# The last 24 token tiles of a routed expert mixture, fetched, mixed and normalised inside the attention layer that follows it

## The chip, the cores and the metric

The kernel runs on one NeuronCore of a Trainium2 chip. The metric is the device time of one execution in microseconds (us). Below, a "tile" is 128 tokens (128 partitions x 128 features, float32), and a "batch" is four tiles.

## What is computed

A post-norm decoder of four layers over 8192 tokens (128 sequences of 64) of width 128. Each of its twelve sublayers ends with a layer norm of the residual sum. The change touches the third and the fourth sublayer:

```python
def _L0_ffn_ref(hidden_states, router_weight, w1, w2):
    ...
    probs = jax.nn.softmax(x @ router_weight, axis=-1)      # 8 experts
    ...                                                     # the top 2 of them keep their probs
    y1, y2 = jnp.split(jnp.einsum('th,ehf->tef', x, w1), 2, axis=-1)
    g = jax.nn.silu(y1) * y2
    o = jnp.einsum('tef,efh->teh', g, w2)
    out = jnp.einsum('teh,te->th', o, local_probs)
def _L1_attn_ref(hidden_states, Wq, Wk, Wv, Wo):            # 16 heads of 64, 4 key/value heads, causal
...
x = _layernorm(x + _L0_ffn_ref(...), axis=-1)
x = _layernorm(x + _L1_attn_ref(...), axis=-1)
```

## The kernel before

All engines are programmed by hand: each has its own instruction list per block, semaphores order them, and a new block starts when every engine has finished the one before. The rows of x live in SBUF (`X`, 64 tiles).

**The mixture** is `routed_experts("L0f", ...)`. Tokens are sorted by expert in three parts of 16, 32 and 16 tiles. For a part, GpSimd scatters the rows of `X` to HBM (`L0f_sorted_x`). Then come 53 expert blocks J of 512 rows (15 + 23 + 15), all written out without a loop: SyncE loads a block's rows and weights (`XB`, `WB`) three blocks ahead, TensorE turns the rows and makes the three first products (L1018, L1020, L1022), ScalarE takes silu, VectorE multiplies the two halves (L1355, twice a block), TensorE makes the second product (L1033), and ScalarE copies the result out and stores it in HBM (`L0f_sorted_y`). Block J's VectorE products free the banks that TensorE needs for the first products of block J+1.

**The tail** brings the results back. When the blocks of a part are stored, GpSimd gathers them, batch by batch: eight indirect DMAs a batch (two experts x four tiles, L959), then the root of the batch before (`root`, L946 and L948: 1/sqrt of the variance). For a batch, VectorE runs `tail_pair(b)`: the shift `nb` of batch b-1 (L1296, waits for that batch's root), two weighted sums a tile into `ACC` (L1304, waits for the gather of b), and the statistics (L1284, L1288). ScalarE writes the normalised rows to `X` (L1082). The table `step_after` says after which block's products VectorE runs which batch: `{25:0, 27:1, 30:2, 32:3, 42:4, 44:5, 47:6, 49:7, 52:8}`. Batches 9 to 15 come after the last block. Part 1 (the second part) holds batches 4 to 11.

**Side work** belongs to later layers (a mask and the statistics of the context, `side_rows` on SyncE and `side_work` on VectorE, L1271 to L1280): eight of its 16 pieces lie beside the blocks of the second part, eight beside the tail after the last block.

**The attention** is `grouped_attention()`. A block of its own loads its four weights and waits for them. Then `pipeline` runs one slot per tile T: scores of T, transposes, values and output product of T-1, while the fills (turning `XS`, making q, k, v) of a coming pair of tiles stand between them. GpSimd copies the rows of a pair to `XS` (L2218) and makes the roots. VectorE has the most to do after TensorE: maximum, shift, copies, the softmax sum and scaling, residual, statistics. The first 8 slots are written out, then 13 turns of a loop hold four slots each, then the rest is written out.

## Time and profile before

| what | value |
|---|---|
| median of 3 runs | 4301.33 us (4296.24 to 4304.2) |
| the profiled execution, its own time | 4300.37 us |
| its span | 4298.6 us |
| TensorE busy / VectorE busy | 3699.6 us (86%) / 3249.1 us (76%) |
| ScalarE busy / GpSimd busy | 2228.5 us (52%) / 1616.4 us (38%) |
| mixture's last block ends on TensorE | 1062.3 us |
| attention begins on TensorE | 1157.2 us |

Busy shares are averages over the whole span; which engine sets the pace differs by stage, so a change in one stage is read from that stage's own rows.

### The profile page before, as it was taken

How to read it: one execution, taken by the hardware profiler on the slowest of the kernel's cores; microseconds unless marked ns; L12 is line 12 of the kernel's file. 1: busy time of each engine (PE TensorE's matmuls, PEld its weight loads, DVE VectorE, ACT ScalarE, POOL GpSimd, SP SyncE). 2: the span in 40 equal slices, each digit the busy share in tenths (PEclk: the TensorE clock that was granted, in tenths of full speed). 3: DMA queues.
4: the chain of work that ended last, by engine and by line, in shares of the span. 5: the costliest groups of instructions: out<-in, count | busy, mean ns of one | idle time of the engine just before them, and what ended most of it. 6: DMA issues, size and time to landing. Idle time of an engine off the chain costs nothing. (4 is left out here: it accounts for less than half of the span.)

```text
span 4298.6 us, 137640 instructions
## 1 busy us (share of the span) xinstructions
PE 3699.6 (86%) x48696; PEld 2734.9 (64%) x48696; DVE 3249.1 (76%) x7860; ACT 2228.5 (52%) x4080; POOL 1616.4 (38%) x2677
## 2 busy tenths in 40 slices
PE   8997998688299998998996858998989687879986
PEld 6775677466177776776776636776764344457764
DVE  7996887344488887887995187997977577769975
ACT  4664553345244443666882445666864354535553
POOL 4663343665411111112454442332223244435544
PEclk9998997899599999999996988999999788989988
DMA  2011112587200000110001840000112000000001
GB/s 78 27 48 38 37 37 62 167 248 188 66 2 0 0 0 11 43 43 28 18 16 58 248 139 13 14 14 30 33 38 64 21 1 0 0 19 24 24 14 39
DMA packets 293808, 209.64 MB, mean 49 GB/s; under 512 B 51137, under 2 KB 272193, under 8 KB 293441
## 3 DMA queue, kind: packets, MB, share of 16 engines
q1 hardware_dynamic: 233760, 157.72, 12.8%
q0 software_dynamic: 12288, 25.19, 2.0%
q10 hardware_dynamic: 47520, 23.60, 1.8%
q8 instruction: 143, 2.34, 0.2%
q14 instruction: 97, 0.79, 0.1%
HBM read 122.49 MB, written 54.53 MB: 41 GB/s over the span
## 5 line engine op out<-in xcount | busy, mean ns | idle before, releaser
L1355 DVE TENSOR_TENSOR L0f_G<-L0f_SG,L0f_psH 128x512 f32<-128x512 f32 x106 | 73.0, 689 | 170.5 <-ACT L0f_SG L1099 127.8
L2224 POOL TENSOR_TENSOR L1a_rs<-L1a_ag,eps 128x1 f32<-128x1 f32 x64 | 12.1, 189 | 476.3 <-DVE L1a_ag L2384 476.3
L938 POOL DMA_INDIRECT L0f_sorted_x<-X,L0f_IDX x128 | 123.1, 961 | 94.1 <-DMA L0f_sorted_x<-X,L0f_IDX 35.7
L959 POOL DMA_INDIRECT L0f_YG<-L0f_sorted_y,L0f_IDY x128 | 124.4, 972 | 69.8 <-issue 35.9
L2311 PE MATMUL L1a_psO<-L1a_WO,L1a_OT 128*64 128x128 f32 x2048 | 125.9, 276 | 6.7 <-ACT L1a_OT L2335 5.7
L2245 PE MATMUL L1a_psF<-L1a_XT,L1a_WQ 128*128 128x256 f32 x512 | 130.8, 389 | 0.5 <-DVE L1a_KT L2200 0.5
L2311 PEld LDWEIGHTS L1a_psO<-L1a_WO,L1a_OT 128*64 128x64 f32 x2048 | 110.6, 137 | 25.2 <-ACT L1a_OT L2335 23.6
L1915 PE MATMUL L3a_psH<-L3a_UT,L3a_WG 128*128 128x512 f32 x128 | 80.9, 718 | 50.1 <-DVE L3a_G L2028 48.6
L1033 PEld LDWEIGHTS L0f_psO<-L0f_WB,L0f_G 128*128 128x128 f32 x848 | 102.9, 192 | 25.5 <-issue 25.5
L586 ACT ACTIVATE L3x_PT<-L3x_psP 128x512 f32<-128x512 f32 x128 | 69.6, 595 | 88.5 <-PE L3x_psP L521 88.5
L586 ACT ACTIVATE L0x_PT<-L0x_psP 128x512 f32<-128x512 f32 x128 | 69.5, 595 | 83.1 <-PE L0x_psP L521 83.1
L2245 PEld LDWEIGHTS L1a_psF<-L1a_XT,L1a_WQ 128*128 128x128 f32 x512 | 93.5, 192 | 23.2 <-DVE L1a_KT L2200 9.7
L1362 DVE TENSOR_TENSOR L1m_YB<-L1m_psO,L1m_WB 128x512 f32<-128x512 f32 x37 | 25.2, 684 | 104.9 <-PE L1m_psO L1033 104.9
L586 ACT ACTIVATE L0a_PT<-L0a_psP 128x512 f32<-128x512 f32 x128 | 69.5, 595 | 65.8 <-PE L0a_psP L521 65.8
L1033 PE MATMUL L0f_psO<-L0f_WB,L0f_G 128*128 128x128 f32 x848 | 103.1, 275 | 0.0
L586 ACT ACTIVATE L2a_PT<-L2a_psP 128x512 f32<-128x512 f32 x128 | 69.6, 595 | 63.3 <-PE L2a_psP L521 63.3
L2329 ACT ACTIVATE L1a_PR<-L1a_PR 128x1024 f32<-128x1024 f32 x64 | 67.6, 1057 | 63.5 <-DVE L1a_PR L2350 63.5
L2324 ACT ACTIVATE L1a_PT<-L1a_psP 128x512 f32<-128x512 f32 x64 | 38.2, 597 | 114.4 <-PE L1a_psP L2288 111.8
L2239 PE MATMUL L1a_psF<-W,L1a_XS 128*128 128x128 f32 x64 | 14.2, 305 | 95.0 <-POOL L1a_XS L2218 94.9
L1982 ACT ACTIVATE L3a_GG<-L3a_psH 128x512 f32<-128x512 f32 x64 | 36.6, 596 | 114.3 <-PE L3a_psH L1916 114.1
L586 ACT ACTIVATE L1x_PT<-L1x_psP 128x512 f32<-128x512 f32 x128 | 69.5, 595 | 45.3 <-PE L1x_psP L521 45.2
L378 POOL TENSOR_TENSOR L1x_rs<-L1x_mv,eps 128x2 f32<-128x2 f32 x32 | 6.2, 195 | 227.6 <-DVE L1x_mv L658 227.6
(684 smaller groups left out, 12996.0 us busy)
## 6 DMA issues: line engine op xcount, KB each, us to landing
L0f_WB<-in_w12a SPq DMA_DIRECT2D x53, 312.0 KB, 3.5
L0f_XB<-L0f_sorted_x SPq DMA_DIRECT2D x53, 256.0 KB, 4.0
L0f_sorted_y<-L0f_YB ACTq DMA_DIRECT2D x53, 256.0 KB
L1m_WB<-in_w12b SPq DMA_DIRECT2D x37, 321.0 KB, 4.0
L1m_XB<-L1m_sorted_x SPq DMA_DIRECT2D x37, 256.0 KB, 3.8
L1m_sorted_y<-L1m_YB ACTq DMA_DIRECT2D x37, 256.0 KB
L0f_sorted_x<-L0f_AC SPq DMA_DIRECT2D x27, 256.0 KB, 4.0
L1m_sorted_x<-L1m_AC SPq DMA_DIRECT2D x27, 256.0 KB, 3.6
```

The source lines that it names most:

```text
L586: nc.scalar.activation(PT[:, A.par, 4 * hb:4 * hb + 4, :], psP[:, hb], ACT.Copy).then_inc(S[done].sem, 1)
L938: nc.gpsimd.indirect_dma_start(out=sorted_x[p][:, :], out_offset=bass.IndirectOffsetOnAxis(ap=IDX[:, k, t:t + 1], axis=0), in_=X[:, t, :], ...
L959: nc.gpsimd.indirect_dma_start(out=YG[:, b % 4, k, t % TB, :], out_offset=None, in_=sorted_y[p][:, :], in_offset=bass.IndirectOffsetOnAxis ...
L1033: m = nc.tensor.matmul(psO[:, J % 2, t, :], G[0:f, J % 2, c, t * P:(t + 1) * P], WB[0:f, J % 4, at:at + D], start=c == 0, stop=c == 1)
L1355: nc.vector.tensor_tensor(G[0:f, J % 2, c, :], SG[0:f, c, :], up, ALU.mult).then_inc(S["g_ready"].sem, 1)
L1362: nc.vector.tensor_tensor(YB[:, J % 3], psO[:, J % 2], along(WB[:, J % 4, 514:514 + D], TB), ALU.add).then_inc(S["expert_out"].sem, 1)
L1915: nc.tensor.matmul(psH[:, c % 2, 0, :], WG[:, c * D:(c + 1) * D], UT[:, A.u, :], start=True, stop=True)
L1982: nc.scalar.activation(GG[:, c % 2, :], psH[:, c % 2, 0, :], ACT.Gelu_apprx_tanh).then_inc(S["gelu"].sem, 1)
L2245: m = nc.tensor.matmul(bank[:, 256 * j:256 * j + 256], WQ[:, 2 * k + j, :], XT[:, N.u, :], start=True, stop=True)
L2311: m = nc.tensor.matmul(psJ[64 * s:64 * s + 64, :], OT[:, s, c, :], WO[:, s, c, :], start=c == 0, stop=c == QC - 1, skip_group_check=True)
L2324: nc.scalar.activation(PT[:, 0:4, :], psP[:, 0], ACT.Copy).then_inc(S["pt_a"].sem, 1)
L2329: nc.scalar.activation(PR[:, T.par], PR[:, T.par], ACT.Exp, scale=scale).then_inc(S["probs"].sem, 1)
```

## The change

The mixture's tail now handles batches 0 to 9 only (`HERE = 10`). The last 24 tiles (`LATER = 24`, tiles 40 to 63) are gathered, summed, normalised and written to `X` one tile at a time in slots -3 to 27 of the attention, by a new class `LateRows` whose pieces stand at the end of each engine's slot. The attention's weights are loaded by SyncE at the end of its list in the mixture; the block that loaded them is gone, and TensorE waits for them before its first slot. All 16 pieces of side work lie beside the blocks. `step_after` becomes `{25:0, 27:1, 30:2, 32:3, 42:4, 44:5, 46:6, 48:7, 50:8, 52:9}`, and the pieces of side work follow blocks 16, 18, 20, 22, 24, 28, 31, 34 to 41 and 43. The attention's written-out part grows from 8 to 32 slots, and its loop has 7 turns.

```diff
+LATER, LATE_FIRST = 24, 32
-def pipeline(eng, slot, ahead=3):
-    first, turns = 8, 13
+def pipeline(eng, slot, ahead=3, first=8):
+    turns = (60 - first) // 4
...
+            HERE = NBATCH - LATER // TB if later is not None else NBATCH
...
-                    if at < BLOCKS:
+                    if at < BLOCKS and b < HERE:
                         step_after[int(at)] = b
-                    at += 2.5 if gated else 2
-            SIDES = NBATCH // 2
+                    at += (2.5 if p == 1 else 2) if gated else 2
+            free = [J for J in range(first[1] + 1, BLOCKS) if J not in step_after]
+            side_after = dict(zip(free[0:14:2] + free[14:], range(NBATCH))) if gated else {}
...
-                        if gated and p == 1 and k % 2 == 0 and k // 2 < SIDES:
-                            side_rows(k // 2)
-                    if gated:
-                        for b in range(SIDES, NBATCH):
-                            side_rows(b)
+                        if J + 1 in side_after:
+                            side_rows(side_after[J + 1])
+                    if later is not None:
+                        later.load_weights(sp)
...
+            def fetch(self, g, T):
+                j = self.tile(T, -3)
+                if j is None:
+                    return
+                t = TILES - LATER + j
+                if j == 0:
+                    for name in ("stored0", "stored1", "stored2"):
+                        g.wait_ge(S[name].sem, S[name].base)
+                self.made(g, "mix", j - 3)
+                for k in range(2):
+                    nc.gpsimd.indirect_dma_start(out=self.YG[:, j % 4, k, :], out_offset=None, in_=self.sorted_y[t >= self.edge][:, :],
+                                                 in_offset=bass.IndirectOffsetOnAxis(ap=self.IDY[:, k, t:t + 1], axis=0)).then_inc(S[f"gathered{j % 4}"].sem, 16)
+            def root(self, g, T):
+                j = self.tile(T, 2)
...
+                self.made(g, "in_stats", j + 1)
+                self.made(g, "late_rows", j - 3)
+                nc.gpsimd.tensor_tensor(self.rt[:, j % 4, 0:1], self.ag[:, j % 4, 1:2], eps[:, 0:1], ALU.add).then_inc(S["in_eps"].sem, 1)
+                self.made(g, "in_eps", j + 1)
+                nc.gpsimd.tensor_tensor(self.rt[:, j % 4, 1:2], self.rt[:, j % 4, 0:1], half[:, 0:1], ALU.pow).then_inc(S["in_rstd"].sem, 1)
+            def mix(self, dv, T):
+                j, a, b = self.tile(T, 0), self.tile(T, 1), self.tile(T, 3)
+                if j is not None:
+                    t = TILES - LATER + j
+                    self.made(dv, f"gathered{j % 4}", 32 * (j // 4 + 1))
+                    self.made(dv, "late_rows", j - 3)
+                    nc.vector.scalar_tensor_tensor(self.ACC[:, j % 4, :], self.YG[:, j % 4, 0, :], self.gate[:, 0, t:t + 1], X[:, t, :], ALU.mult, ALU.add).then_inc(S["own"].sem, 1)
+                if a is not None:
...
+                    nc.vector.bn_aggr(self.ag[:, a % 4, :], self.st[:, a % 2, :]).then_inc(S["in_stats"].sem, 1)
+                if j is not None:
+                    self.made(dv, "own", j + 1)
+                    nc.vector.scalar_tensor_tensor(self.ACC[:, j % 4, :], self.YG[:, j % 4, 1, :], self.gate[:, 1, t:t + 1], self.ACC[:, j % 4, :], ALU.mult, ALU.add).then_inc(S["mix"].sem, 1)
+                if b is not None:
+                    self.made(dv, "in_rstd", b + 1)
...
+                if j is not None:
+                    self.made(dv, "mix", j + 1)
+                    nc.vector.bn_stats(self.st[:, j % 2, :], self.ACC[:, j % 4, :]).then_inc(S["in_bn"].sem, 1)
+            def rows(self, act, T):
+                j = self.tile(T, 4)
...
+                self.made(act, "late_shift", j + 1)
+                nc.scalar.activation(X[:, TILES - LATER + j, :], self.ACC[:, j % 4, :], ACT.Identity, scale=self.rt[:, j % 4, 1:2], bias=self.nb[:, j % 4:j % 4 + 1]).then_inc(S["late_rows"].sem, 1)
...
-            with nc.Block() as block:
-                @block.sync
-                def _(sp):
-                    for d, s_ in ((WQ[:, :, :], io["wq"]), (WK[:, :, :], io["wk"]), (WV[:, :, :, :], io["wv"]), (WO[:, 0, :, :], io["wo"]), (WO[0:64, 1, :, :], io["wo"][64:128]), (WO[64:128, 1, :, :], io["wo"][0:64])):
-                        sp.dma_start(d, s_).then_inc(S["weights_in"].sem, 16)
-                    sp.wait_ge(S["weights_in"].sem, S["weights_in"].base + 96)
...
+                        later.root(g, T)
+                        later.fetch(g, T)
+                    pipeline(g, slot, 3, LATE_FIRST)
...
+                    pe.wait_ge(S["grouped_in"].sem, S["grouped_in"].base + 96)
+                    pipeline(pe, slot, 2, LATE_FIRST)
...
+                        later.rows(act, T)
...
+                        later.mix(dv, T)
```

`self.tile(T, back)` gives j = slot number - back, so a tile's gather stands in slot j-3, its sums in slot j, its statistics' aggregate in slot j+1, its root (GpSimd) in slot j+2, its shift in slot j+3 and its rows (ScalarE) in slot j+4.

Three places show how instructions move. The first is GpSimd at the start of the attention. Before, right after the branch into the block (the three copies are those of pairs 0, 1 and 2):

```order
L946 TENSOR_TENSOR L0f_rt<-L0f_ag,eps 128x4
L948 TENSOR_TENSOR L0f_rt<-L0f_rt,half 128x4
L870 UNCONDITIONAL_BRANCH
L2210 UNCONDITIONAL_BRANCH
L2218 COPY L1a_XS<-X 128x256 x3
L2224 TENSOR_TENSOR L1a_rs<-L1a_ag,eps 128x1
```

Now (`LYG` receives a late tile's two expert rows, `Lrt` is its root):

```order
L955 TENSOR_TENSOR L0f_rt<-L0f_rt,half 128x4
L878 UNCONDITIONAL_BRANCH
L2289 UNCONDITIONAL_BRANCH
L1432 DMA L1a_LYG<-L0f_sorted_y,rest_IDY 128x128 x2
L2298 COPY L1a_XS<-X 128x256
L1432 DMA L1a_LYG<-L0f_sorted_y,rest_IDY 128x128 x4
L2298 COPY L1a_XS<-X 128x256
L1432 DMA L1a_LYG<-L0f_sorted_y,rest_IDY 128x128 x4
L2298 COPY L1a_XS<-X 128x256
L2304 TENSOR_TENSOR L1a_rs<-L1a_ag,eps 128x1
L2306 TENSOR_TENSOR L1a_rs<-L1a_rs,half 128x1
L1441 TENSOR_TENSOR L1a_Lrt<-L1a_Lag,eps 128x1
```

Two gathers stand ahead of the first copy to `XS`, and four ahead of each of the next two.

The second is VectorE at the end of an attention slot. Before, from the residual sum of one tile to the maximum of the next slot:

```order
L2373 TENSOR_SCALAR X<-L1a_RB,L1a_ag,L1a_rs 128x128
L2379 TENSOR_TENSOR L1a_RB<-L1a_psO,X 128x128
L2381 BN_STATS L1a_st<-L1a_RB 128x6
L2384 BN_AGGR L1a_ag<-L1a_st 128x2
L2346 TENSOR_REDUCE L1a_mx<-L1a_psS 128x16
```

Now, in one of the slots with the full late work:

```order
L2458 TENSOR_SCALAR X<-L1a_RB,L1a_ag,L1a_rs 128x128
L2464 TENSOR_TENSOR L1a_RB<-L1a_psO,X 128x128
L2466 BN_STATS L1a_st<-L1a_RB 128x6
L2469 BN_AGGR L1a_ag<-L1a_st 128x2
L1451 SCALAR_TENSOR_TENSOR L1a_LACC<-L1a_LYG,rest_gate,X 128x128
L1455 BN_AGGR L1a_Lag<-L1a_Lst 128x2
L1458 SCALAR_TENSOR_TENSOR L1a_LACC<-L1a_LYG,rest_gate,L1a_LACC 128x128
L1462 SCALAR_TENSOR_TENSOR L1a_Lnb<-L1a_Lag,L1a_Lrt 128x1
L1465 BN_STATS L1a_Lst<-L1a_LACC 128x6
L2431 TENSOR_REDUCE L1a_mx<-L1a_psS 128x16
```

Five instructions of a late tile stand between the aggregate and the next maximum.

The third is VectorE at the end of the expert blocks. Before, from block 49's products to block 52's (the last):

```order
L1355 TENSOR_TENSOR L0f_G<-L0f_SG,L0f_psH 128x512
L1355 TENSOR_TENSOR L0f_G<-L0f_SG,L0f_psH 48x512
L1296 SCALAR_TENSOR_TENSOR L0f_nb<-L0f_ag,L0f_rt 128x4
L1304 SCALAR_TENSOR_TENSOR L0f_ACC<-L0f_YG,L0f_gate,X 128x128 x4
L1304 SCALAR_TENSOR_TENSOR L0f_ACC<-L0f_YG,L0f_gate,L0f_ACC 128x128 x4
L1284 BN_STATS L0f_st<-L0f_ACC 128x6 x4
L1288 BN_AGGR L0f_ag<-L0f_st 128x2 x4
L1355 TENSOR_TENSOR L0f_G<-L0f_SG,L0f_psH 128x512
L1355 TENSOR_TENSOR L0f_G<-L0f_SG,L0f_psH 48x512
L1355 TENSOR_TENSOR L0f_G<-L0f_SG,L0f_psH 128x512
L1355 TENSOR_TENSOR L0f_G<-L0f_SG,L0f_psH 48x512
L1355 TENSOR_TENSOR L0f_G<-L0f_SG,L0f_psH 128x512
```

Now, from block 50's products (the first row is the second of its pair) to those of block 52:

```order
L1364 TENSOR_TENSOR L0f_G<-L0f_SG,L0f_psH 48x512
L1305 SCALAR_TENSOR_TENSOR L0f_nb<-L0f_ag,L0f_rt 128x4
L1313 SCALAR_TENSOR_TENSOR L0f_ACC<-L0f_YG,rest_gate,X 128x128 x4
L1313 SCALAR_TENSOR_TENSOR L0f_ACC<-L0f_YG,rest_gate,L0f_ACC 128x128 x4
L1293 BN_STATS L0f_st<-L0f_ACC 128x6 x4
L1297 BN_AGGR L0f_ag<-L0f_st 128x2 x4
L1364 TENSOR_TENSOR L0f_G<-L0f_SG,L0f_psH 128x512
L1364 TENSOR_TENSOR L0f_G<-L0f_SG,L0f_psH 48x512
L1364 TENSOR_TENSOR L0f_G<-L0f_SG,L0f_psH 128x512
L1364 TENSOR_TENSOR L0f_G<-L0f_SG,L0f_psH 48x512
L1305 SCALAR_TENSOR_TENSOR L0f_nb<-L0f_ag,L0f_rt 128x4
```

Batch 7, which stood behind block 49, now stands behind block 48; batch 8 moves from block 52 to block 50, and batch 9 from after the blocks to block 52.

## Rows read from the trace of the kernel before

**Rows 1.** Busy time of each engine in three stretches: blocks, gap, attention.
```profile
core 0: us, PE busy (x) PEld busy (x) DVE busy (x) ACT busy (x) POOL busy (x), PEclk, DMA share, GB/s
960.00:1062.30 102.30, 102.29 (x560) 71.43 (x558) 50.87 (x147) 54.90 (x104) 52.80 (x58) 1.00 0.75 200
1062.30:1157.20 94.90, 0.00 (x0) 0.00 (x0) 39.55 (x209) 16.96 (x41) 59.23 (x69) 0.51 0.33 85
1183.22:1223.90 40.68, 40.68 (x711) 32.52 (x711) 35.72 (x55) 19.75 (x33) 4.41 (x12) 1.00 0.01 3
```

**Rows 2.** Timeline of TensorE: start, length, instruction, idle before and its releaser.
```profile
1042.88 1.02 PE L1020 MATMUL L0f_psH<-L0f_XT,L0f_WB 128*128 128x512 f32 x2
...
1058.56 3.73 PE L1033 MATMUL L0f_psO<-L0f_WB,L0f_G 128*128 128x128 f32 x32
1157.21 0.69 PE L2239 MATMUL L1a_psF<-W,L1a_XS 128*128 128x128 f32 x2 [94.92 <-POOL L1a_XS L2218]
```

**Rows 3.** Timeline of GpSimd: roots of batches 6, 7, 8, gathers, first copy.
```profile
1042.55 1.03 POOL L948 TENSOR_TENSOR L0f_rt<-L0f_rt,half 128x4 f32<-128x4 f32 x1
...
1054.67 1.03 POOL L948 TENSOR_TENSOR L0f_rt<-L0f_rt,half 128x4 f32<-128x4 f32 x1
1055.90 1.00 POOL L959 DMA_INDIRECT L0f_YG<-L0f_sorted_y,L0f_IDY  x1 [0.19 <-issue]
1057.21 0.96 POOL L959 DMA_INDIRECT L0f_YG<-L0f_sorted_y,L0f_IDY  x1 [0.30 <-issue]
...
1066.07 1.04 POOL L948 TENSOR_TENSOR L0f_rt<-L0f_rt,half 128x4 f32<-128x4 f32 x1
...
1156.76 0.73 POOL L2218 COPY L1a_XS<-X 128x256 f32<-128x256 f32 x2 [12.36 <-SPq L2209]
```

**Rows 4.** Timeline of VectorE: block products and the sums of batches 9 and 15.
```profile
1040.66 1.41 DVE L1355 TENSOR_TENSOR L0f_G<-L0f_SG,L0f_psH 128x512 f32<-128x512 f32 x2 [0.53 <-ACT L0f_SG L1099]
1044.00 0.69 DVE L1355 TENSOR_TENSOR L0f_G<-L0f_SG,L0f_psH 128x512 f32<-128x512 f32 x1 [1.93 <-ACT L0f_SG L1099]
...
1067.14 0.16 DVE L1296 SCALAR_TENSOR_TENSOR L0f_nb<-L0f_ag,L0f_rt 128x4 f32<-128x4 f32 x1 [3.45 <-POOL L0f_rt L948]
1067.46 1.14 DVE L1304 SCALAR_TENSOR_TENSOR L0f_ACC<-L0f_YG,L0f_gate,X 128x128 f32<-128x128 f32 x4 [0.16 <-DMA L0f_YG<-L0f_sorted_y,L0f_IDY]
...
1139.41 1.14 DVE L1304 SCALAR_TENSOR_TENSOR L0f_ACC<-L0f_YG,L0f_gate,X 128x128 f32<-128x128 f32 x4
```

**Rows 5.** Timeline of VectorE: one whole step of the tail, batch 7.
```profile
1046.03 0.15 DVE L1296 SCALAR_TENSOR_TENSOR L0f_nb<-L0f_ag,L0f_rt 128x4 f32<-128x4 f32 x1
1046.10 1.13 DVE L1304 SCALAR_TENSOR_TENSOR L0f_ACC<-L0f_YG,L0f_gate,X 128x128 f32<-128x128 f32 x4
...
1048.44 0.87 DVE L1284 BATCH_NORM_STATS2 L0f_st<-L0f_ACC 128x6 f32<-128x128 f32 x4
1049.35 0.38 DVE L1288 BATCH_NORM_AGGREGATE L0f_ag<-L0f_st 128x2 f32<-128x6 f32 x4
```

**Rows 6.** Timeline: the mixture's last rows on ScalarE, the weights' first load on SyncE.
```profile
1144.73 1.65 ACT L1082 ACTIVATE X<-L0f_ACC,L0f_nb,L0f_rt 128x128 f32<-128x128 f32 x4 [3.66 <-DVE L0f_nb L1296]
...
1147.34 0.35 SPq L2171 DMA_DIRECT2D L1a_WQ<-in_wq  x1
```

**Rows 7.** Who waited for whom, 1180 to 1690 us: total, times, longest.
```profile
DVE L1a_OT L2358 <- PE L1a_psO L2302: 33.3, 61, 0.9
```

**Rows 8.** The attention's maximum on VectorE by tile: durations, first, last; its waits.
```profile
L2346 DVE TENSOR_REDUCE L1a_mx<-L1a_psS x64: 1191/1224/1226, 1168.7 to 1683.0; 128x16 f32<-128x1024 f32 x64
...
  issue: 4.4, 13
```

**Rows 9.** By tile or line, min/median/max: sums, mask work (ns), gathers' landing.
```profile
L1304 DVE SCALAR_TENSOR_TENSOR L0f_ACC<-L0f_YG,L0f_gate,X x64: 334/343/360, 932.4 to 1140.2; 128x128 f32<-128x128 f32 x64
...
L1271 DVE TENSOR_SCALAR maskk<-L0f_MK x16: 258/281/348, 890.5 to 1144.6; 128x256 bf16<-128x256 int32 x16
...
DMA to landing us min/median/max: 2.5/3.2/5.0
```

More of the change, by code:

```diff
@@ L825, in routed_experts @@
             RK, RS, MV = mem.sb("RK", [P, GT, NE]), mem.sb("RS", [P, GT, NE]), mem.sb("MV", [P, max(PARTS), NE])
-            carry, counts, gate = mem.sb("carry", [P, NG + 1, NE]), mem.sb("counts", [P, len(PARTS), NE]), mem.sb("gate", [P, top, TILES])
+            carry, counts = mem.sb("carry", [P, NG + 1, NE]), mem.sb("counts", [P, len(PARTS), NE])
+            gate = later.gate if later is not None else mem.sb("gate", [P, top, TILES])
             PLACE, MOVE = mem.sb("PLACE", [P, top, TILES]), mem.sb("MOVE", [P, TILES])
-            IDX, IDY = (mem.sb(n, [P, top, TILES], mybir.dt.uint32) for n in ("IDX", "IDY"))
+            IDX = mem.sb("IDX", [P, top, TILES], mybir.dt.uint32)
+            IDY = later.IDY if later is not None else mem.sb("IDY", [P, top, TILES], mybir.dt.uint32)
+            if later is not None:
+                later.sorted_y = sorted_y[-2:]
+                later.edge = part_tile[-2]
             CNT, NBK, ENDS, SH = (mem.sb(n, [P, NE]) for n in ("CNT", "NBK", "ENDS", "SH"))
@@ L1355, in _ @@
                                 nc.vector.tensor_tensor(G[0:f, J % 2, c, :], SG[0:f, c, :], up, ALU.mult).then_inc(S["g_ready"].sem, 1)
[L1356 to L1358 removed]
+                            if J in side_after:
+                                side_work(side_after[J])
                         else:
@@ L2213, in slot @@
                         N, A = T + 2, T - 2
+                        later.all_rows(g, T)
                         if T.par == 0 and N.ok:
@@ L2342, in slot @@
                         A, E = T - 1, T - 2
+                        later.all_rows(dv, T)
                         if T.ok:
@@ L2398, in build @@
                   bo=R("L0xb"), cross=True, norm="rms")
-        routed_experts("L0f", 2, "w12a", "rwa")
-        grouped_attention()
+        rest = Memory(nc, "rest")
+        later = LateRows(rest)
+        routed_experts("L0f", 2, "w12a", "rwa", later=later)
+        grouped_attention(later)
+        rest.close()
         attention("L1x", Wm("L1xq"), Wm("L1xk"), Wm("L1xv"), Wm("L1xo"), bq=C("L1bq"), bk=C("L1bk"), bo=rowb[:, 0, :],
```

74 lines of the change are left out of this document (50 added, 24 removed).

## The prediction

> **What bounds the kernel now.** I read the stage windows first. In the last 100 us of the expert blocks TensorE is busy throughout; then it does nothing for 94.9 us, with its granted clock down to 0.51; in the attention it is busy all the time again at clock 1.00 [rows 1]. TensorE's timeline says the same at the edges: its last block instruction ends at 1062.29, its next starts at 1157.21, and the releaser is GpSimd's copy to `XS` [rows 2]. So whatever shortens this gap comes off the end, and whatever lengthens an attention slot is added to it.
>
> What fills the gap is read from GpSimd, the engine that is busiest in it (59.2 us of 94.9) [rows 1]. A gather's start follows the last by 1.26 us (a busy 0.96 and 0.30 of issue), and a batch's eight gathers with its root take some 11.3 us: the roots of batches 6, 7 and 8 end at 1043.6, 1055.7 and 1067.1 [rows 3]. Batches 9 to 15 follow each other at this pace, VectorE's sums of batch 9 start at 1067.46 and those of batch 15 at 1139.41 [rows 4], and ScalarE's last rows end at 1146.38 [rows 6]. Then SyncE starts the weights' loads at 1147.34 [rows 6] and the first copy to `XS` at 1156.76 has waited for them [rows 3].
>
> In the attention VectorE is busy 35.7 of 40.7 us [rows 1]. Its one regular wait is for TensorE's value product before the copy to `OT`: 33.3 us in 61 slots, 0.55 us each [rows 7]. A slot takes (1683.0 - 1168.7) / 63 = 8.16 us [rows 8]. VectorE thus has about 0.55 us to spare in a slot, plus little.
>
> **Removed: batches 10 to 15 and the weights' block.** GpSimd's chain up to the gather of batch 9 stays where it is. VectorE's step for batch 9 then starts at 1067.46 as before, held by the root of batch 8 and the landing of the gather [rows 4]. From the start of a last batch's sums to the end of ScalarE's rows it took 1146.38 - 1139.41 = 6.97 us (sums, statistics, root, shift, rows) [rows 4, 6]. So the mixture ends at 1067.46 + 6.97 = 1074.4. Changing blocks takes 1147.34 - 1146.38 = 0.96 us [rows 6], which gives 1075.4. Now two gathers of 1.26 us stand ahead of the first copy: 1077.9. TensorE starts 0.45 us behind the copy (1156.76 to 1157.21) [rows 2, 3]: 1078.4. That is **78.8 us** earlier than 1157.21. The next two copies have four gathers ahead of them each (5 us). TensorE turned pair 1 more than 11 us after pair 0, because pair 0's fills lie between, so the second is hidden; the third waits for the sums of slot 0 and two gathers, and I give it 4 us of room; should it be late, each us counts once.
>
> **Moved: weights and side work beside the blocks.** The weights' loads are issued after the last block's operands, with more than 20 us before TensorE asks for them; taken as nothing. Eight more pieces of side work fall behind blocks 34 to 43; a piece has a mask conversion of 0.28 us [rows 9] and four statistics and aggregates like those of a tail step, 0.87 + 0.38 us [rows 5], so some 1.6 us. VectorE is busy 50.9 of 102.3 us there, and the window's 560 matmuls, 26 a block, make a block 4.8 us [rows 1]. A pair of block products may be late: the pair of block 48 ran at 1040.66 to 1042.07, behind a tail step, and TensorE's product of block 49, which needs it, began at 1042.88 without a wait [rows 2, 4]. Block 49's own pair began at 1044.00 [rows 4], so block 48's was due at 1039.2; to be done before 1042.88 and before the following product's need at 1043.7, the pair can begin as late as 1042.1, 2.9 us late. 1.6 us of side work fits. But it brings 384 KB more DMA into a period of 4.8 us (80 GB/s on top of 200, where the DMA share is 0.75 already [rows 1]), which can delay the store of the second part's last block, and with it all gathers. I take 1 us; bounds 0 and 4.
>
> **Moved: tail steps two blocks apart instead of 2.5.** VectorE's order puts a wait inside the blocks. Two blocks last 9.6 us, GpSimd's batch 11.3 us. Step 7 now stands behind block 48 (products due at 1039.2 to 1041.3), but needs the root of batch 6 (1043.6 [rows 3]) and the gather of batch 7, whose last DMA starts 1.5 us ahead of that root's 1042.55 and lands 2.5 to 5.0 us after its start [rows 3, 9], so at 1043.6 to 1046. So it starts at about 1045 and lasts 3.7 us (1046.03 to 1049.73 [rows 5]), until 1048.7. Block 49's products, due at 1044.0 [rows 4] and free to be 2.9 us late, push TensorE by 1.8 us. Step 8 behind block 50 waits likewise to 1057 and ends at 1060.8; block 51 (due at 1053.6 + 1.8) pushes 2.5 us more. The blocks end about 4.4 us later, at 1066.7. VectorE's step for batch 9 cannot start before 1067.4 anyway, so this is hidden by GpSimd's chain, with under 3 us of room on VectorE (block 52's second product pair ends at 1064.5). Cost 0; were the cover gone, each further us of slip counts once. Bounds 0 and 5.
>
> **Added: the late tile in a slot.** On VectorE: two sums at 1.13 / 4 = 0.28 us, statistics at 0.87 / 4 = 0.22, aggregate 0.10, shift 0.07 to the next start, and two dependent starts at 0.04 [rows 5]: 1.04 us a slot, for 24 slots (four more have only a part). If VectorE's waits for the value product close entirely, a slot grows by 1.04 - 0.55 = 0.49 us. If none is absorbed, it is 1.04, or 25 us; if VectorE also wins its small gaps, 0.35, or 8 us. The copies that VectorE makes for TensorE come later too, and TensorE then waits for some of them, but both grow by the same slot. I take 0.5: **+12 us**. On ScalarE one activation of a tile (1.65 / 4 = 0.41 us [rows 6]) joins 19.8 busy us of 40.7 [rows 1]: nothing. GpSimd gets two gathers and a root, 2.5 + 1.1 us, in a slot where it is busy 0.9 us: nothing. A tile's gather is issued three slots (24 us) before its sums, and lands within 5 us [rows 9].
>
> **Loop turns.** VectorE waited 4.4 us for issue at 13 turns [rows 8], 0.34 us each; six turns fewer, and part of it was TensorE's slack: -1 us (bounds 0 and -2).
>
> **Sum.** -78.8 + 1 + 12 - 1 = -66.8 us. Against the profiled execution's 4300.4 us this is 4233.6; the median of the runs shown is 0.9 us above that execution, well inside their scatter of 8 us. I predict 4234 us.
>
> **A rule that speaks against it.** Beside the gathers, VectorE's sums took 334 to 360 ns and the mask's conversion 258 to 348 ns [rows 9]: GpSimd's gathers hold VectorE up by no more than 0.09 us. The Trainium skill (SBUF — State Buffer, "Who interferes with whom") says that VectorE and GpSimd share a port pair as an exclusive lock, so that an instruction with two SBUF inputs, or a copy in a two-port mode, and a GpSimd instruction block each other for their whole length. By that rule each gather could hold VectorE for its 0.96 us; the rows here do not show it for gathers, and I keep their durations.
>
> **Rivals.**
> - *All of the late work lands on the path* (0.8 to 1.1 us a slot): VectorE becomes the bound and TensorE's fills wait for its copies, which wait behind the late work. For it: VectorE is already at 88% in a slot. Against it: the 0.55 us of wait. 4300.4 - 78.8 + 19 to 26 = 4241 to 4248 (the other two terms cancel). Chance 0.17.
> - *Cheaper than I think* (0.15 to 0.35 a slot): 4 to 8 us instead of 12, 4225 to 4230. Chance 0.09.
> - *The blocks slip beyond their cover* (side work's DMAs, two late steps): 3 to 8 us are exposed, 4237 to 4242. Chance 0.08.
> - *GpSimd's gathers block VectorE* in its long two-input multiplication: up to 2 x 0.96 us a slot, 24 slots: 46 us, 4280. Rows 9 speak against it. Chance 0.04.
> - *Slower: the gather comes too late for its sums.* If GpSimd, held by its waits for statistics and sums at a slot's end, issued a tile's gathers only one slot ahead of need, VectorE would stand in every slot for two gathers and a landing, 2.5 + 1.5 to 4 us. From 78.8 / 24 = 3.3 us a slot on, the gain is gone; at 4.5 it is 4300 + 30 = 4330. Against it: the waits in slot c ask for what VectorE made in slot c-1, and 24 us of lead. Chance 0.03.
> - *No gain*: the start of the attention stays bound by something that the gap hid. Nothing in the rows shows one. Chance 0.01.
>
> **How the numbers follow.** The forecast, 4229 to 4241, has 0.58. The 8-in-10 range takes in the cheaper case, the slipping blocks and the full price of the late work: 4224 to 4251. A measurement of this kernel can tell about 0.2% (9 us) from no change. "Slower" is 0.03; no gain is the same, and so is a small part of the blocking case at its worst: 0.02. The rest, 0.95, is faster.
>
> **What would show it.** TensorE's idle time before the first `XS` turn falls from 94.9 to about 12 us, with the turn at about 1078. VectorE shows waits for roots or gathers behind blocks 48 and 50, of 2 to 4 us. In the first 24 slots the period is 8.6 to 8.7 us, VectorE's wait before `OT` is all but gone, and later slots are back at 8.16. The prediction is wrong if the turn comes after 1085, if the period is beyond 9.2, or if VectorE waits for `LYG`.

## The result, and the profile after

The changed kernel takes 4257.7 us (median of 4 runs, 4250.0 to 4259.4) against 4301.2 us before: a ratio of 0.9896 with a 95% interval of 0.9879 to 0.9914. It is faster by about 44 us, or 1.0%. The prediction had said 67 us (4234, range 4224 to 4251), so the sign was right and the time lies outside the range. The profiled executions stand at 4300.37 and 4259.36 us, 41.1 us apart in their spans.

Windows of the changed kernel, with the columns of [rows 1]: the last expert blocks, the gap, attention slots with late work, slots without.
```profile
960.00:1077.34 117.34, 110.86 (x588) 75.92 (x586) 75.00 (x275) 60.03 (x116) 59.48 (x67) 0.97 0.83 227
1077.34:1094.80 17.46, 0.00 (x0) 0.01 (x1) 0.85 (x7) 5.43 (x13) 3.59 (x5) 0.61 0.11 31
1114.00:1300.00 186.00, 176.86 (x3046) 140.39 (x3046) 175.55 (x338) 90.56 (x161) 77.74 (x135) 1.00 0.06 17
1340.00:1600.00 260.00, 257.87 (x4560) 207.02 (x4555) 229.40 (x350) 123.52 (x209) 28.97 (x80) 1.00 0.00 1
```
The gap of 94.9 us [rows 1] is down to 17.5, but the blocks now end at 1077.3 instead of 1062.3. In the slots with late work VectorE is busy 175.55 of 186 us, and TensorE is no longer busy all the time.

TensorE's timeline in the changed kernel: its first instruction of the mixture, blocks 51 and 52, the first turn of `XS`, and the first instruction after the attention.
```profile
706.25 0.69 PE L980 MATMUL L0f_psX<-W,X 128*128 128x128 f32 x2 [6.85 <-DMA L0f_TRI<-in_tri]
...
1069.31 2.08 PE L1029 MATMUL L0f_psH<-L0f_XT,L0f_WB 128*128 128x512 f32 x2 [6.38 <-DVE L0f_G L1364]
...
1072.89 4.45 PE L1042 MATMUL L0f_psO<-L0f_WB,L0f_G 128*128 128x128 f32 x32
1094.82 0.66 PE L2321 MATMUL L1a_psF<-W,L1a_XS 128*128 128x128 f32 x2 [17.48 <-POOL L1a_XS L2298]
...
1651.21 0.69 PE L435 MATMUL L1x_psF<-W,L1x_XS 128*128 128x128 f32 x2 [6.60 <-POOL L1x_XS L410]
```
Two of the same places before.
```profile
702.02 0.47 PE L971 MATMUL L0f_psX<-W,X 128*128 128x128 f32 x1 [6.84 <-DMA L0f_TRI<-in_tri]
...
1698.24 0.44 PE L434 MATMUL L1x_psF<-W,L1x_XS 128*128 128x128 f32 x2 [3.01 <-POOL L1x_XS L409]
```
The mixture began 4.2 us later in the changed kernel's execution, in code that is the same up to there. So stages have to be compared from their own starts, and "on the clock of before" means a time of the changed kernel less these 4.2 us. From the mixture's first instruction to the first turn it took 1157.21 - 702.02 = 455.2 us before and 1094.82 - 706.25 = 388.6 after: 66.6 us saved. The attention, from the first turn to the end of its last product, took 538.0 and takes 549.8. The gap behind it was 3.01 and is 6.60. The sum by stages:

| stage | predicted | measured |
|---|---|---|
| mixture's start to the first turn of `XS` | -77.8 | -66.6 |
| attention | +11 | +11.8 |
| gap behind the attention | 0 | +3.6 |
| stages whose code is the same (ahead +4.2, behind +5.9) | 0 | +10.1 |
| span | -66.8 | -41.1 |

The last row but one is scatter. The largest part of it is the second mixture on TensorE, 239.7 us before and 246.0 after; in the other kernels of this study, with the same code there, it took between 239.1 and 248.8, and 248.8 in one that is otherwise the kernel before. The largest part ahead of the mixture is the sublayer just before it on TensorE (347.8 and 352.0), which took 348 to 353 in the others.

VectorE's timeline at the end of the blocks: steps 7 and 8, blocks 51 and 52, step 9.
```profile
1048.50 0.16 DVE L1305 SCALAR_TENSOR_TENSOR L0f_nb<-L0f_ag,L0f_rt 128x4 f32<-128x4 f32 x1 [1.29 <-POOL L0f_rt L955]
...
1060.03 0.16 DVE L1305 SCALAR_TENSOR_TENSOR L0f_nb<-L0f_ag,L0f_rt 128x4 f32<-128x4 f32 x1 [3.20 <-POOL L0f_rt L955]
1064.90 1.14 DVE L1313 SCALAR_TENSOR_TENSOR L0f_ACC<-L0f_YG,rest_gate,X 128x128 f32<-128x128 f32 x4 [4.70 <-DMA L0f_YG<-L0f_sorted_y,rest_IDY]
...
1073.76 0.69 DVE L1364 TENSOR_TENSOR L0f_G<-L0f_SG,L0f_psH 48x512 f32<-48x512 f32 x1 [1.58 <-ACT L0f_SG L1108]
...
1074.44 1.13 DVE L1313 SCALAR_TENSOR_TENSOR L0f_ACC<-L0f_YG,rest_gate,X 128x128 f32<-128x128 f32 x4
...
1081.80 0.16 DVE L1305 SCALAR_TENSOR_TENSOR L0f_nb<-L0f_ag,L0f_rt 128x4 f32<-128x4 f32 x1 [3.74 <-POOL L0f_rt L955]
```
ScalarE and GpSimd from there to the attention (`LYG` is the first late gather), in the timeline.
```profile
1077.38 0.60 ACT L1076 ACTIVATE L0f_YB<-L0f_psO 128x512 f32<-128x512 f32 x1 [1.19 <-PE L0f_psO L1042]
...
1078.69 4.96 ACT L1091 ACTIVATE X<-L0f_ACC,L0f_nb,L0f_rt 128x128 f32<-128x128 f32 x12 [0.72 <-ACT L0f_YB L1076]
```
```profile
1080.48 0.20 POOL L953 TENSOR_TENSOR L0f_rt<-L0f_ag,eps 128x4 f32<-128x4 f32 x1 [9.04 <-ACT X L1091]
1080.76 1.01 POOL L955 TENSOR_TENSOR L0f_rt<-L0f_rt,half 128x4 f32<-128x4 f32 x1
1091.98 1.01 POOL L1432 DMA_INDIRECT L1a_LYG<-L0f_sorted_y,rest_IDY  x1 [10.21 <-SPq L2288]
```
Step 8 waited 3.2 us for a root and then 4.7 us more for its gather, and blocks 51 and 52 stood behind it. GpSimd's last root had to wait for the rows of batch 7, whose buffer it writes again (9.04 us idle, until 1080.4), and these stood in ScalarE's queue behind the work for blocks 51 and 52. The twelve rows in ScalarE's timeline are those of batches 7, 8 and 9, four each. ScalarE's last rows end at 1083.65, but GpSimd begins the attention only at 1091.98. What it does meanwhile stands among its sequencer's own instructions, grouped by line (durations in ns, shortest, median and longest of the two mixtures): the first mixture's is the one at 1080.7.
```profile
L878 POOLq DRAIN  x2: 10278/12614/14950, 1080.7 to 2517.3; - x2
```
```profile
L2288 POOLq DRAIN  x1: 4589/4589/4589, 1645.9 to 1645.9; - x1
```
The same before, at the first mixture's end and at the attention's end:
```profile
L870 POOLq DRAIN  x2: 3745/9266/14788, 1143.4 to 2557.3; - x2
```
```profile
L2209 POOLq DRAIN  x1: 662/662/662, 1696.5 to 1696.5; - x1
```
### The profile page after: what moved, and what is told of

It reads as the page before. It is cut to its first block and busy times, and to the rows that moved or that the text cites. A ratio compares the mean times of both kernels' runs of the same rounds, so it can differ in the third digit from the quotient of the medians.

```text
span 4257.5 us, 137131 instructions
## 1 busy us (share of the span) xinstructions
PE 3716.0 (87%) x48696; PEld 2745.1 (64%) x48696; DVE 3256.5 (76%) x7878; ACT 2228.5 (52%) x4080; POOL 1635.3 (38%) x2713
## 5 line engine op out<-in xcount | busy, mean ns | idle before, releaser
L945 POOL DMA_INDIRECT L0f_sorted_x<-X,L0f_IDX x128 | 123.6, 965 | 93.0 <-DMA L0f_sorted_x<-X,L0f_IDX 34.6
L2393 PE MATMUL L1a_psO<-rest_WO,L1a_OT 128*64 128x128 f32 x2048 | 127.5, 278 | 10.4 <-ACT L1a_OT L2418 8.6
L2327 PE MATMUL L1a_psF<-L1a_XT,rest_WQ 128*128 128x256 f32 x512 | 131.0, 390 | 0.5 <-DVE L1a_KT L2279 0.5
L2393 PEld LDWEIGHTS L1a_psO<-rest_WO,L1a_OT 128*64 128x64 f32 x2048 | 112.1, 138 | 29.7 <-ACT L1a_OT L2418 28.9
L2327 PEld LDWEIGHTS L1a_psF<-L1a_XT,rest_WQ 128*128 128x128 f32 x512 | 93.8, 193 | 23.1 <-issue 9.7
L2412 ACT ACTIVATE L1a_PR<-L1a_PR 128x1024 f32<-128x1024 f32 x64 | 67.7, 1057 | 74.3 <-DVE L1a_PR L2435 74.3
L968 POOL DMA_INDIRECT L0f_YG<-L0f_sorted_y,rest_IDY x80 | 78.1, 976 | 55.0 <-DMA L0f_sorted_y<-L0f_YB 28.2
L945 POOL DMA_INDIRECT L1m_sorted_x<-X,L1m_IDX x64 | 61.7, 964 | 77.1 <-DMA L1m_sorted_x<-X,L1m_IDX 39.9
```

Source lines behind the costliest of these rows:

```text
L945: nc.gpsimd.indirect_dma_start(out=sorted_x[p][:, :], out_offset=bass.IndirectOffsetOnAxis(ap=IDX[:, k, t:t + 1], axis=0), in_=X[:, t, :], ...
L968: nc.gpsimd.indirect_dma_start(out=YG[:, b % 4, k, t % TB, :], out_offset=None, in_=sorted_y[p][:, :], in_offset=bass.IndirectOffsetOnAxis ...
L2327: m = nc.tensor.matmul(bank[:, 256 * j:256 * j + 256], WQ[:, 2 * k + j, :], XT[:, N.u, :], start=True, stop=True)
L2393: m = nc.tensor.matmul(psJ[64 * s:64 * s + 64, :], OT[:, s, c, :], WO[:, s, c, :], start=c == 0, stop=c == QC - 1, skip_group_check=True)
L2412: nc.scalar.activation(PR[:, T.par], PR[:, T.par], ACT.Exp, scale=scale).then_inc(S["probs"].sem, 1)
```

## The experiments

Each kernel ran beside the kernel before, not beside the changed kernel, in three sets whose medians of before were 4304.3, 4307.5 and 4307.8 us (4301.2 beside the changed kernel). So whole times of different sets are compared by their ratios, and only where the intervals do not overlap is a difference of whole times shown. Numbers of the stages are those of the one profiled execution of each kernel: M is the time from TensorE's first instruction of the mixture to the attention's first turn of `XS` (455.2 before, 388.6 changed), B the part of it from the first gather of batch 9 on (34.6 changed), which leaves out how late the chain of gathers began. With side rows two blocks ahead and with gathers alone, which leave the end of the mixture as it is, B is 33.8 and 34.4, so it scatters by about 1 us. The attention with all the work on 24 late tiles took 547.3 to 549.8 us, whatever else was edited.

**Drains in idle places.**
```diff
+                        if gated and p:
+                            nc.gpsimd.drain()
                         made(g, "cut", p + 1)
...
                         later.fetch(g, T)
+                        if T.i is None and T.c == 29:
+                            nc.gpsimd.drain()
```

> The changed kernel, with a drain of GpSimd of its own in three idle places: before it waits for the stores of the second and of the third part, and in attention slot 29, after the last late tile. Then only 48 gathers are left at the mixture's end: GpSimd's idle time before its first late gather falls from 10.21 to about 5 us, TensorE's first turn of XS comes 5 us earlier, the gap after the attention is back at 3.0 us, the whole is 8 to 9 us faster than the changed kernel (about 4249). Theory B: the hold is the longer code being fetched, or the block's barrier: both gaps stay as they are (10.2 and 6.6 us), the time stays at 4258 or grows by the added drains.

Measured: 4243.2 us (4240.8 to 4250.3), ratio to before 0.9857 (0.9840 to 0.9873) against the changed kernel's 0.9896 (0.9879 to 0.9914), which is 17 us where 8 to 9 were expected. The stages of the profiled execution show 3.9 us in the mixture, 3.6 behind the attention, and 2.5 in the attention, which is within its scatter; what is left of the 17 lies within the width of the intervals. M 384.7, B 28.2. Only one of the two drains in the tail exists, since the third part has no gathers there. GpSimd's timeline and TensorE's after the attention:
```profile
1085.11 1.01 POOL L1434 DMA_INDIRECT L1a_LYG<-L0f_sorted_y,rest_IDY  x1 [4.97 <-SPq L2290]
```
```profile
1638.30 0.44 PE L435 MATMUL L1x_psF<-W,L1x_XS 128*128 128x128 f32 x2 [3.02 <-POOL L1x_XS L410]
```
Both holds shrank as theory A said, 10.21 to 4.97 and 6.60 to 3.02 us; theory B falls. The added drains, in idle time, took 6.35 us (with 160 scatters and gathers issued) and 4.57 us (with 48):
```profile
L961 POOLq DRAIN  x1: 6350/6350/6350, 974.0 to 974.0; - x1
```
```profile
L2312 POOLq DRAIN  x1: 4574/4574/4574, 1346.3 to 1346.3; - x1
```

**Side rows two blocks ahead.**
```diff
-                        if J + 1 in side_after:
-                            side_rows(side_after[J + 1])
+                        if J + 2 in side_after:
+                            side_rows(side_after[J + 2])
```

> The changed kernel, with the rows of a piece of side work issued by SyncE two blocks ahead of their use instead of one. Theory A: the blocks slip because VectorE waits for these rows (0.65 to 2.93 us at nearly every piece between 980 and 1027) and because the stores and gathers come late: the waits vanish, GpSimd's first gather of batch 4 starts 1 to 2 us earlier, the blocks' end on TensorE comes 1 to 3 us earlier, and the attention's start 1 to 3 us. Theory B: VectorE has the room for these waits, and the slip comes from the two late tail steps alone: the waits vanish, and the blocks end within 0.5 us of where they ended, the time within 1 us.

Measured: 4255.1 us (4250.0 to 4260.5), 0.9882 (0.9865 to 0.9900), as the changed kernel within the scatter. VectorE's waits for these rows between 960 and 1015 are gone; in the changed kernel they were 15.6 us in 8 pieces, in this row of its trace:
```profile
DVE maskk L1280 <- DMA L0f_CH<-in_ctx: 15.6, 8, 2.9
```
B is 33.8, about as before the edit, and in the profiled execution M rose to 395.4, as the chain of gathers began 7 us later: a tail step beside the second part's blocks had waited 2.9 us for its gather and TensorE 2.7 us for the products behind it. So the waits for the side rows cost nothing, and both theories missed the later start of the chain. Batch 4's gathers begin 305.3 us after the mixture's start here and 297 to 301 in all the other kernels (before 296.9, changed 298.3). Whether the earlier loads brought this on or it is scatter is not shown: it is one execution, and the median did not rise.

**Weights first.**
```diff
+                    if later is not None:
+                        later.load_weights(sp)
                     for e in range(NE):
                         fill(0, e)
...
                             side_rows(side_after[J + 1])
-                    if later is not None:
-                        later.load_weights(sp)
```

> The changed kernel, with the attention's weights loaded at the start of the mixture, before the expert blocks, instead of beside the last two blocks. Theory A: the weights' 1.8 MB between 1053 and 1065 hold up the landing of batch 8's gather (VectorE waited 4.70 us for it, 6.2 us after its last DMA was issued), so that blocks 51 and 52 slip: without them the wait falls to 1 to 2 us, blocks 51 and 52 come 3 us earlier, the tail's last step 2 to 4 us earlier, and the whole is 2 to 4 us faster. Theory B: the landing is slow for another reason (the batch's own 512 KB beside block rows): wait 4 to 5 us as before, time unchanged.

Measured: 4253.5 us (4243.0 to 4256.0), 0.9884 (0.9868 to 0.9901). Step 8 on VectorE:
```profile
1061.95 1.14 DVE L1313 SCALAR_TENSOR_TENSOR L0f_ACC<-L0f_YG,rest_gate,X 128x128 f32<-128x128 f32 x4 [1.09 <-DMA L0f_YG<-L0f_sorted_y,rest_IDY]
```
The wait for the landing is 1.1 us instead of 4.7, the blocks end 3.5 us earlier from the mixture's start (367.6 instead of 371.1), B is 29.5 instead of 34.6, M 386.1. By these stages theory A holds: the weights' loads were not free. The whole time alone would not show it, as its interval overlaps the changed kernel's. GpSimd's idle time before the first late gather is 10.21 us again.

**The old spacing.**
```diff
-                    at += (2.5 if p == 1 else 2) if gated else 2
+                    at += 2.5 if gated else 2
```

> The changed kernel, with the tail steps of the third part again 2.5 blocks apart (batch 6 behind block 47, 7 behind 49, 8 behind 52, 9 after the blocks), everything else as changed. Theory A: the closer spacing costs, because each wait for a root or a gather inside the blocks pushes TensorE: with the old spacing the blocks end on TensorE 8 to 10 us earlier (about 1067 to 1069), batch 9's sums start at about 1071.7 instead of 1074.4, the mixture's rows end 3 to 5 us earlier; the whole is 3 to 5 us faster. Theory B, the prediction's: GpSimd's chain covers the slip, the rows end within 1 us of the changed kernel's, the time stays.

Measured: 4250.2 us (4245.7 to 4253.4), 0.9873 (0.9857 to 0.9890). The blocks end 10.1 us earlier from the mixture's start (361.0 instead of 371.1), B is 29.8, M 384.1. Theory A, again by the stages (the intervals of the whole times overlap). GpSimd's idle time is 10.22 us, and its drain 10.28 us, as in the changed kernel.

**Gathers alone in the attention.** Edit: `later.mix` (VectorE), `later.root` (GpSimd) and `later.rows` (ScalarE) are taken out, and a gather waits for the landing of the one four tiles earlier instead of its sums.

> The changed kernel with the late gathers kept in the attention but everything that is made of them left out there (the two sums, statistics, aggregate, shift, root and rows), so that the last 24 tiles of x are not mixed and not normalised. Read is the attention on TensorE, from its first turn of XS to its last product: 538.0 us before, 549.8 changed. Theory A: the 11.8 us are VectorE's own time for the late tiles, less its slack: without it the attention takes 536 to 539 us, and the period of the first 24 slots is 8.16. Theory B: GpSimd's 48 gathers hold VectorE up, at up to 0.96 us each: the attention keeps most of the 11.8 us and a period near 8.6.

**Plain loads instead of gathers.**
```diff
-                    nc.gpsimd.indirect_dma_start(out=self.YG[:, j % 4, k, :], out_offset=None, in_=self.sorted_y[t >= self.edge][:, :],
-                                                 in_offset=bass.IndirectOffsetOnAxis(ap=self.IDY[:, k, t:t + 1], axis=0)).then_inc(S[f"gathered{j % 4}"].sem, 16)
+                    g.dma_start(self.YG[:, j % 4, k, :], self.sorted_y[t >= self.edge][(2 * j + k) * P:(2 * j + k + 1) * P, :]).then_inc(S[f"rows_in{j % 4}"].sem, 16)
...
+                @block.sync
+                def _(sp):
+                    for name in ("stored0", "stored1", "stored2"):
+                        sp.wait_ge(S[name].sem, S[name].base)
+                    for c in range(-3, LATER - 3):
+                        later.fetch(sp, At(None, c))
```

> The changed kernel with the late tiles' rows loaded by plain DMAs of SyncE (of the same size, in the order of the sorted rows, so that wrong rows are summed) instead of GpSimd's gathers; all other late work is kept. Theory A (VectorE's own time is the price): the attention on TensorE stays at 547 to 550 us, with a period of 8.6 in the slots with late work; only its start is about 2.3 us earlier, as no gathers stand ahead of the first copy to XS, and the gap behind it is back at 3.0 us, as there are no gathers to drain. Theory B (gathers hold VectorE up): it falls to 538 to 542 us.

Measured, one execution each, 4230.0 and 4244.3 us. On TensorE the attention takes 536.8 us with gathers alone and 547.4 with plain loads (before 538.0, changed 549.8). From its first maximum to its last it is 514.1 and 524.1 us; before 514.3, changed 525.7. The rows by tile, of the changed kernel, of gathers alone, and of plain loads:
```profile
L2431 DVE TENSOR_REDUCE L1a_mx<-L1a_psS x64: 1191/1224/1226, 1106.6 to 1632.3; 128x16 f32<-128x1024 f32 x64
```
```profile
L2430 DVE TENSOR_REDUCE L1a_mx<-L1a_psS x64: 1190/1223/1225, 1102.4 to 1616.5; 128x16 f32<-128x1024 f32 x64
```
```profile
L2436 DVE TENSOR_REDUCE L1a_mx<-L1a_psS x64: 1189/1223/1226, 1098.4 to 1622.5; 128x16 f32<-128x1024 f32 x64
```
The period of slots 1 to 24 is 8.24 and 8.64 us in the two (8.22 before, 8.63 changed). So the price of the attention is the work on the late tiles, and GpSimd's 48 gathers add nothing to it: theory A in both. Gathers alone also lacks the late work of ScalarE and GpSimd; that VectorE's part is the price rests on VectorE's own time, told below. With plain loads the gap behind the attention is 3.02 us, as there is nothing to drain, and the turn comes 8.3 us behind the mixture's last rows instead of 11.2.

**Longer code before.** The kernel before with `first = 32` in the attention's `pipeline`, and nothing else.

> The kernel before, with 32 slots of the attention written out instead of 8 and 7 turns of its loop instead of 13, and nothing else. By the prediction the attention takes 1 us less (537 instead of 538.0; bounds 0 and 2). Theory B: longer code costs, and the attention takes 1 us or more longer; the start of the attention block also comes later then.

Measured, one execution: the attention takes 538.6 us (538.0 before). Neither theory: writing out 24 more slots changed nothing that shows. The whole was at 4312.4, of which 9.1 us are the second mixture (248.8).

**The mends together.**
```diff
-            with nc.Block() as block:                      # the mixture's
+            with nc.Block(no_gpsimd_drain=gated) as block:
...
+                        if T.i is None and T.c in (3, 29):
+                            nc.gpsimd.drain()
```
with the drain while waiting, the weights first and the old spacing as above.

> The changed kernel with the three mends together: the weights loaded at the start of the mixture, the third part's tail steps 2.5 blocks apart, and GpSimd's drain taken off the mixture's end (its block closes without one; GpSimd drains while it waits for the stores of the second and third part, and at the end of attention slots 3 and 29). Theory A (the three losses are apart and add up): from TensorE's first instruction of the mixture to the attention's first turn it takes 374 to 378 us instead of 388.6, the gap after the attention is 3.0 instead of 6.6 us, the attention itself stays at 547 to 550; together 14 to 18 us off the changed kernel, 4240 to 4245 us. Theory B: behind each mended loss lies the next one (the gather chain or another engine's block end), and the mixture takes 382 to 384 us, as with one mend alone.

> The combined kernel once more, beside the two with more late tiles, to see how far its unchanged stages scatter. Expected: 4237 to 4244 us again, the mixture from TensorE's first instruction to the attention's first turn 376 to 380 us.

Measured: 4240.3 us (4236.2 to 4243.6), 0.9847 (0.9826 to 0.9868), and in the second go 4242.6 (4237.6 to 4243.2), 0.9844 (0.9828 to 0.9859). M 378.4 and 378.0, B 22.4 and 22.2, the attention 549.6 and 549.8, the gap behind it 3.0. The timeline of VectorE, ScalarE and GpSimd at the mixture's end:
```profile
1072.31 1.14 DVE L1315 SCALAR_TENSOR_TENSOR L0f_ACC<-L0f_YG,rest_gate,X 128x128 f32<-128x128 f32 x4 [0.19 <-DMA L0f_YG<-L0f_sorted_y,rest_IDY]
```
```profile
1077.54 1.65 ACT L1093 ACTIVATE X<-L0f_ACC,L0f_nb,L0f_rt 128x128 f32<-128x128 f32 x4 [3.73 <-DVE L0f_nb L1307]
```
```profile
1080.25 1.01 POOL L1434 DMA_INDIRECT L1a_LYG<-L0f_sorted_y,rest_IDY  x1 [2.94 <-SPq L2290]
...
1082.53 0.41 POOL L2300 COPY L1a_XS<-X 128x256 f32<-128x256 f32 x1
```
From the last sums to the last rows it is 1079.19 - 1072.31 = 6.9 us, from there to the first late gather 1.1, to the copy 2.3 more. This is nearer theory A, with M at and just above the end of its 374 to 378, and against the changed kernel's ratio of 0.9896 the whole time is clearly shorter. But only two of the losses add up. B fell by some 12.3 us: 7.3 of them are GpSimd's idle time (2.94 instead of 10.21), and 5.0 are what weights first or the old spacing gives alone. From the first gather of batch 9 to the last rows it took 23.5 us in the changed kernel, 18.3 with weights first, 18.6 with the old spacing and 18.5 and 18.3 with both: either one is enough, and behind it GpSimd's chain is the bound.

**More late tiles.** The combined kernel with `LATER, LATE_FIRST = 28, 36` and `32, 40`; in the latter the attention also waits for 20 of the late rows in slot 30.

> The combined kernel with 28 late tiles (batch 9 goes to the attention, 36 slots are written out, drains in slots 3 and 33). Four more late tiles cost 1.7 us in the attention. Theory A: the gather of batch 9 and its sums, 11.3 us on GpSimd, fall away from the end of the tail, and the attention starts 6 to 9 us earlier than in the combined kernel (370 to 372 us after the mixture's first instruction): 4 to 7 us faster. Theory B: the last block and its store hold the end at 374 or later: 0 to 3 us faster.

> The combined kernel with 32 late tiles instead of 24 (batches 8 and 9 go to the attention too; 40 of its slots are written out, and GpSimd's drains stand in slots 3 and 37). A late tile costs 0.41 to 0.45 us on its slot (measured: 8.63 to 8.69 us instead of 8.22), so eight more cost 3.3 to 3.6 us. What they save is bounded by the blocks: the combined kernel's last block ends 362 us after the mixture's first instruction and the attention starts at 378. Theory A: without batches 8 and 9 the tail no longer sets the end, the attention starts 4 to 6 us behind the last block plus its store, at 368 to 372, and the whole is 3 to 7 us faster than the combined kernel. Theory B: what is left behind the last block (store, rows in ScalarE's queue, block change, gathers before the first copy) takes 12 us or more, and the two kernels are within 2 us of each other.

Measured: 28 tiles 4233.5 us (4226.9 to 4240.0), 0.9823 (0.9807 to 0.9840); 32 tiles 4234.6 us (4234.4 to 4238.1), 0.9832 (0.9817 to 0.9847). M 371.9 and 370.3, the attention 552.4 and 552.3. Their medians are 8 to 9 us under that of the combined kernel run beside them, but the intervals of all three overlap, and the stages give only 3.5 us (28 tiles) and 5.2 (32). Both intervals lie clear of the changed kernel's 0.9896; the two are not told apart. The start came as theory A had it in both: with 28 tiles 6.1 us earlier, with 32 only 1.6 us earlier still, 8.2 us behind the last block, which ends at 362 us in both.

Each of these kernels has a drain in slot 3 and one behind the last late tile (slot 29, 33 or 37), with different numbers of gathers issued since the last drain (24, 28 and 32 late tiles):
```profile
L2312 POOLq DRAIN  x2: 3432/5782/8131, 1119.7 to 1343.8; - x2
```
```profile
L2312 POOLq DRAIN  x2: 4087/5784/7482, 1114.9 to 1372.4; - x2
```
```profile
L2314 POOLq DRAIN  x2: 4737/5780/6824, 1108.6 to 1400.4; - x2
```
The two records of a kernel cannot be set side by side as they stand, since a drain's record begins while older instructions are still to run. GpSimd's timeline with 24 tiles has the root and both gathers of slot 3 inside the drain that began at 1119.74:
```profile
1119.78 0.55 POOL L1445 TENSOR_TENSOR L1a_Lrt<-L1a_Lrt,half 128x1 f32<-128x1 f32 x1
1120.50 0.99 POOL L1434 DMA_INDIRECT L1a_LYG<-L0f_sorted_y,rest_IDY  x1 [0.17 <-issue]
1121.80 0.96 POOL L1434 DMA_INDIRECT L1a_LYG<-L0f_sorted_y,rest_IDY  x1 [0.31 <-issue]
1127.96 0.39 POOL L2300 COPY L1a_XS<-X 128x256 f32<-128x256 f32 x1 [5.20 <-issue]
```
So the gathers since the last drain were 62, 54 and 46 in slot 3 (48, 40 and 32 in the mixture's tail and 14 in the attention) and 34, 42 and 50 in the later one. From the end of the last older instruction to the end of the drain it took 5.12, 4.47 and 3.82 us, and 2.85, 3.50 and 4.15. All six lie on one line: 0.08 us and 0.081 us for each gather.

## Why the prediction was wrong, point by point

- **Removed: batches 10 to 15 and the block.** The reading of GpSimd's chain was right: the root of batch 8 ended 365.2 us after the mixture's start, where it had been 365.1 [rows 3]. "Changing blocks takes 0.96 us" **failed**, and it is the largest part of the miss. The 0.96 between ScalarE's last rows and SyncE's load [rows 6] was what remained of a drain of 3.7 us that had begun 3 us before those rows ended; after the change the drain was 10.3 us and began 2.9 us before. The hold was 1091.98 - 1083.65 = 8.3 us, 7.4 more than predicted.
- **Moved: the weights, "taken as nothing"**, and **tail steps two blocks apart, hidden: 0.** Both failed, together. Step 7 started its sums at 1049.10, 1044.9 on the clock of before, as forecast (about 1045). Step 8 was forecast to wait until 1057 and end at 1060.8; it started its sums at 1064.90, which on the clock of before (4.2 us less) is 1060.7, since its gather landed late beside the weights' 1.8 MB. The slip was 10.8 us at the blocks' end instead of 4.4, more than the cover of "under 3 us of room" beyond it, and then ScalarE's queue (the work for blocks 51 and 52, batch 7's rows) stood ahead of the last root, so that it took 9.2 us from the last sums to the rows instead of 6.97. From the mixture's start the rows ended at 377.4 instead of 373.4 us: 4.0 us. Weights first or the old spacing each took 5 us off B, and both together no more.
- **Moved: side work, +1.** Batch 4's gathers began 1.4 us later than before from the mixture's start. The DMAs did come late (15.6 us of waits on VectorE, the longest 2.9), but TensorE stayed busy for all 55 us between 960 and 1015, and loading them earlier changed nothing in B. So the room for late products was real.
- **The combined kernel is the check of this part.** From the last sums to the rows 6.9 us (predicted 6.97), to the gather 1.1 (0.96), then 2.8 to the turn (2.97). By the predicted steps the turn comes 1078.4 + 1 - 702.0 = 377.4 us after the mixture's start; measured 378.0 and 378.4. So the steps were right once the drain was out of the block's end. The 0.96 us was right there by luck: it had been read from a drain, and the kernel that it fits has none on GpSimd.
- **Added: the late tile, +12.** Measured 11.8 for the attention. The period grew by 8.63 - 8.22 = 0.41 us, forecast 0.5; VectorE's busy time in a slot rose from 7.24 to 8.16 us (forecast 1.04 more, measured 0.92), and its idle time fell from 0.96 to 0.49. Most of that is the wait before `OT`, from some 0.55 to 0.18 us a slot (the row behind this point, for the window from 1120 to 1310), in place of rows 7. The sums take 0.35 us instead of 0.28. The missing 2 us came back at the start (slot 0 takes 7.27 instead of 6.29) and in the last slots. Right mechanism, and the size within 0.1 us a slot. VectorE never waited for `LYG`, and later slots took 8.18 us (forecast 8.16).

```profile
DVE L1a_OT L2443 <- PE L1a_psO L2384: 4.0, 11, 0.4
```

- **Loop turns, -1:** failed as a term; it is +0.6 in the one execution, which is no difference that shows.
- **The rule on the shared port.** The Trainium skill (SBUF — State Buffer, "Who interferes with whom") has a VectorE instruction with two SBUF inputs contend with a GpSimd instruction that reads SBUF; it also infers that generating descriptors needs the shared write interface, which such a `tensor_tensor` does not take. The prediction left this limit out. Gathers alone and plain loads agree with rows 9 against a price for gathers: 0.02 us a slot at most (8.24 against 8.22, 8.64 against 8.63).
- **The rivals.** "The blocks slip beyond their cover" was the right one in kind, with 4 us inside its 3 to 8; the drain, the other 11 us, was in none. Of the 26 us missing in the profiled execution, 15.6 are the change's (11.2 in the mixture, 3.6 behind the attention, 0.8 in it) and 10.1 the scatter of stages that it does not touch. Without these it would stand at 4249.2, just inside the range; the range had taken in neither the drain nor the scatter of single stages, and the median of 4257.7 lies outside. The prediction's own sign of being wrong, a turn after 1085, came true: 1094.8, or 1090.6 on the clock of before.
